# Edge-scoring stage of a graph and expert network: earlier source gathers, and duplicate search and weight sums outside the edge loop

## What is computed

```python
x1 = x[edges[0]]
x2 = x[edges[1]]
e = jnp.concatenate([x1, x2], axis=1) @ Ww + bw
e = e.reshape(-1, H, 2 * HD).transpose(1, 0, 2)
e = jax.nn.leaky_relu(e, 0.01)
w = (e @ Wa + ba)[..., 0]
mat = jnp.full((H, n, n), -jnp.inf, jnp.float32)
mat = mat.at[:, edges[0], edges[1]].set(w)
mat = jax.nn.softmax(mat, axis=-1)
```

## Time and profile before

| | |
|---|---|
| median of 3 runs | 830.37 us (829.98 to 833.03) |
| profiled execution, own time | 826.04 us |
| its span, first to last instruction | 824.3 us |
| PE / DVE / POOL busy | 77% / 62% / 25% of the span |
| granted TensorE clock, mean | 0.864 of full speed |
| DMA moved | 208.07 MB, mean 252 GB/s |

### The profile page before, as it was taken

The page is one execution under the profiler, slowest core; times in us unless marked ns, Lnnn a source line. Parts: engine busy times, 40 slices in busy tenths (PEclk is TensorE's granted clock), DMA queues, the critical chain, the costliest instruction groups (busy, mean ns, idle before and its releaser), DMA issues.

```text
span 824.3 us, 9492 instructions
## 1 busy us (share of the span) xinstructions
PE 637.2 (77%) x2879; PEld 317.8 (39%) x2879; DVE 507.3 (62%) x1437; ACT 252.8 (31%) x1072; POOL 202.8 (25%) x223
## 2 busy tenths in 40 slices
PE   4972345533334938998989999889999999999966
PEld 2431112211113934455455545444444444444422
DVE  3377999889887997547473244774449644443512
ACT  2104776555662332345232010211111111211211
POOL 6047677777772000000000000011101101101100
PEclk9995556755555878999999999999999999999998
DMA  8688878787875709704000002378999999999981
GB/s 330 248 309 319 299 253 261 251 261 261 260 252 195 249 29 410 249 1 154 0 1 1 0 0 77 125 325 357 422 421 421 420 421 423 420 423 421 422 362 42
DMA packets 46645, 208.07 MB, mean 252 GB/s; under 512 B 7969, under 2 KB 12577, under 8 KB 37120
## 3 DMA queue, kind: packets, MB, share of 16 engines
q1 hardware_dynamic: 27296, 145.70, 43.7%
q0 software_dynamic: 19296, 61.75, 22.1%
HBM read 199.67 MB, written 10.31 MB: 255 GB/s over the span
## 4 chain that ended last, share of the span: by engine, by line
PE 60%; DMA 14%; DVE 13%; POOL 5%; issue 5%; ACT 2%; SPq 0%; POOLq 0%; DVEq 0%
PE bank L853 14%; PE bank L543 8%; PE bank L873 6%; PE bank L891 5%; DMA score<-late,e_i 4%; PE bank L741 4%; PE bank L756 4%; DVE R L1324 3%; PE bank L657 3%; POOL R L454 2%; PE bank L650 2%; DMA R<-L_w 2%; DMA R<-tok_tab,slot_tok 2%; DMA R<-tab_src,e_i 2%; POOL R L447 2%
## 5 line engine op out<-in xcount | busy, mean ns | idle before, releaser
L992 ACT ACTIVATE R<-R 128x128 f32<-128x128 f32 x384 | 113.0, 295 | 98.7 <-DVE R L1328 98.7
L591 PE MATMUL bank<-R 128*128 128x384 bf16 x144 | 50.5, 486 | 117.3 <-DVE R L1287 117.3
L853 PE MATMUL bank<-R 128*64 128x512 f32 (+1 forms) x432 | 107.2, 611 | 9.5 <-DMA R<-L_w 8.4
L496 POOL DMA_INDIRECT R<-tok_tab,slot_tok x33 | 33.0, 1000 | 248.7 <-DVE slot_f L1711 203.2
L1723 DVE TENSOR_TENSOR R<-R,bank 128x256 f32<-128x256 f32 x34 | 14.3, 421 | 109.0 <-ACT R L1105 109.0
L543 PE MATMUL bank<-R,late 128*128 128x512 f32 x168 | 77.4, 620 | 2.2 <-DMA R<-L_Ww 2.2
L992 ACT ACTIVATION_READ_ACCUMULATOR R<-R 128x1 f32 x384 | 71.6, 186 | 0.0
L591 PEld LDWEIGHTS bank<-R 128*128 128x128 bf16 x144 | 13.3, 119 | 149.9 <-DVE R L1287 140.9
L1324 DVE TENSOR_TENSOR R<-R 128x1032 f32<-128x1032 f32 x48 | 59.1, 1232 | 17.2 <-DMA R<-tab_src,e_i 10.5
L485 POOL MEMSET R<- 128x512 f32 x3 | 1.6, 525 | 242.4 <-DVEq L1642 242.3
L1328 DVE SCALAR_TENSOR_TENSOR R<-R,sm 128x1024 f32<-128x1024 f32 x48 | 59.1, 1231 | 1.7
(11 more groups left out here) (374 smaller groups left out, 1093.4 us busy)
## 6 DMA issues: line engine op xcount, KB each, us to landing
R<-L_w SPq DMA_DIRECT2D x54, 1536.0 KB, 15.1
late<-L_w SPq DMA_DIRECT2D x18, 1536.0 KB, 15.3
R<-L_w SPq DMA_DIRECT2D x2, 3072.0 KB, 15.4
score<-R POOLq DMA_DIRECT2D x9, 512.0 KB, 12.3
R<-L_Ww SPq DMA_DIRECT2D x2, 2048.0 KB, 13.9
R<-L_W SPq DMA_DIRECT2D x4, 1024.0 KB, 9.2
R<-score SPq DMA_DIRECT2D x2, 1536.0 KB, 10.9
tab_src<-R SPq DMA_DIRECT2D x3, 516.0 KB, 3.8
```

Source lines behind the costliest of these rows:

```text
L496: pool.indirect_dma_start(out=xg[j], out_offset=None, in_=tok_tab[:, :], in_offset=bass.IndirectOffsetOnAxis(ap=slot_tok[:, i:i + 1], axis=0),
L591: last = pe.matmul(pb[s][:, 0:N], oh[:, e % 2, 0, P * s:P * s + P], oh[:, e % 2, 1, :], start=(e == 0), stop=(e == ET - 1))
L853: last = pe.matmul(pb[4 + i % 2][part, :], xeT[i % 2][:, k, part], w13[e % NWB][:, k, :], start=(k == 0), stop=(k == KD - 1), tile_positio ...
L992: act_.activation(own, own, ACT.Copy, accum_out=w_e3[:, t, h:h + 1]).then_inc(S("heads_summed"), 1)
```

## The change

Five more source buffers come out of the `late` tiles (`NGF` = 18), and 16 source gathers (`NEARLY`) are issued ahead of the wait for the destination table. The key products and the duplicate search become functions, `keys(g)` and `seek_duplicates(g)`. Groups 0 and 1 are done within the source table's first tile, groups 2 to 4 between the destination table and the loop, groups 5 to 11 in the loop as before. The two weight sums stand after the counts. The buffer that serves as source for filling the score matrix is now the eighteenth.

```diff
--- before.py
+++ after.py
@@ -32,8 +32,9 @@
 ROUND = 1.5 * 2.0 ** 23
 SLOPE = 0.01
 ROW = 2 * D + H
-NGF = 13
-NEARLY = 9
+NGF = 18
+NEARLY = 16
+DUP_TABLE, DUP_EARLY = 2, 5
 NGD = 6
 V_FROM = 4
 NWB = 11
@@ -149,6 +150,7 @@
         lsc = prod[0]
         ab = [R2[:, 2560 + ROW * j:2560 + ROW * j + ROW] for j in range(NT)]
         ga = [r1(10240 + ROW * j, ROW) for j in range(7)] + [R2[:, 12288 + ROW * j:12288 + ROW * j + ROW] for j in range(6)]
+        ga += [late[0][:, ROW * j:ROW * j + ROW] for j in range(3)] + [late[1][:, ROW * j:ROW * j + ROW] for j in range(2)]
         gd = [r1(ROW * j, ROW) for j in range(NGD)]
         mt = [r1(3072 * j, 3072).rearrange("p (n h) -> p n h", h=H) for j in range(NT)]
 
@@ -550,6 +552,15 @@
 
             pe.wait_ge(S("consts_ready"), 1)
 
+            def keys(g):
+                if g >= 2:
+                    pe.wait_ge(S("dup_used"), g)
+                for j in range(4):
+                    e, o = 4 * g + j, pb[6 + g % 2][:, P * j:P * j + P]
+                    pe.matmul(o, src_h[:, e:e + 1].to_broadcast([P, P]), ident16[:, 0:P], start=True, stop=False)
+                    last = pe.matmul(o, dst_h[:, e:e + 1].to_broadcast([P, P]), ident16[:, P:2 * P], start=False, stop=True)
+                last.then_inc(S("key_psum"), 1)
+
             for t in range(NT):
                 transposes("1", t).then_inc(S("xT_psum"), 1)
             for t in range(NT):
@@ -560,26 +571,23 @@
                     if t:
                         pe.wait_ge(S("src_half_ready"), 2 * (t - 1) + half + 1)
                     project(t, 3 + half, xT, Ww[:, 0:4, D * half:D * half + D]).then_inc(S("src_rows_psum"), 1)
+                    if t == 0:
+                        if half == 0:
+                            pe.wait_ge(S("edge_idx_ready"), 1)
+                        keys(half)
             pe.wait_ge(S("Ww_loaded_dst"), 32)
             for t in range(NT):
                 for half in range(2):
                     if t:
                         pe.wait_ge(S("dst_half_ready"), 2 * (t - 1) + half + 1)
                     project(t, (5, 0)[half], xT, Ww[:, 4:8, D * half:D * half + D]).then_inc(S("dst_rows_psum"), 1)
-            pe.wait_ge(S("edge_idx_ready"), 1)
+            for g in range(DUP_TABLE, DUP_EARLY):
+                keys(g)
             pe.wait_ge(S("src_half_ready"), 2 * NT)
             pe.wait_ge(S("dst_half_ready"), 2 * NT)
             for e in range(ET):
-                if e % 4 == 0:
-
-                    g = e // 4
-                    if g >= 2:
-                        pe.wait_ge(S("dup_used"), g)
-                    for j in range(4):
-                        o = pb[6 + g % 2][:, P * j:P * j + P]
-                        pe.matmul(o, src_h[:, e + j:e + j + 1].to_broadcast([P, P]), ident16[:, 0:P], start=True, stop=False)
-                        last = pe.matmul(o, dst_h[:, e + j:e + j + 1].to_broadcast([P, P]), ident16[:, P:2 * P], start=False, stop=True)
-                    last.then_inc(S("key_psum"), 1)
+                if e % 4 == 0 and e // 4 >= DUP_EARLY:
+                    keys(e // 4)
                 if e % 4 == 2 and V_FROM <= e // 4 < V_FROM + NT:
                     v = e // 4 - V_FROM
                     if v == 0:
@@ -1261,10 +1269,32 @@
                     ins = ts(share, share, bias, None, ALU.add)
                 ins.then_inc(ready, 1)
 
+            dup_scr, dup0_f = dup_s, V_("dup0_f", ET // 4)
+
+            def seek_duplicates(g):
+                t = 4 * g
+                dve.wait_ge(S("key_psum"), g + 1)
+                keys = pb[6 + g % 2]
+                for j in range(4):
+                    e = t + j
+                    lo = P * (j - 1) if j else 0
+                    go(stt(dup_scr[:, 256 * j:256 * j + P * (j + 1) - lo], keys[:, lo:P * (j + 1)], key_f[:, e:e + 1],
+                           before_s[:, 0:2 * P] if j else tri, ALU.is_equal, ALU.mult, accum_out=dup_f[:, e:e + 1]))
+                if g:
+                    go(stt(dup_scr[:, P:2 * P], pb[7 - g % 2][:, 3 * P:4 * P], key_f[:, t:t + 1], ones,
+                           ALU.is_equal, ALU.mult, accum_out=dup0_f[:, g:g + 1]))
+                    settle()
+                    go(tt(dup_f[:, t:t + 1], dup_f[:, t:t + 1], dup0_f[:, g:g + 1], ALU.add))
+                settle()
+                stt(row_i[:, t:t + 4], dup_f[:, t:t + 4], 262144.0, key_f[:, t:t + 4], ALU.mult, ALU.add).then_inc(S("dup_used"), 1)
+                dve.wait_ge(S("dup_used"), g + 1)
+
             for t in range(NT):
                 for half in range(2):
                     dve.wait_ge(S("src_half_ready"), 2 * t + half + 1)
                     linear_part(ab[t], half, S("src_rows_ready"))
+                    if t == 0:
+                        seek_duplicates(half)
             for t in range(NT):
                 dve.wait_ge(S("src_rows_stored"), 16 * NT)
                 dve.wait_ge(S("Ww_loaded_dst"), 32)
@@ -1273,8 +1303,9 @@
                     tt(ab[t][:, D * half:D * half + D], pb[(5, 0)[half]][:, :], bwr[:, D * half:D * half + D], ALU.add).then_inc(S("dst_half_ready"), 1)
                     dve.wait_ge(S("dst_half_ready"), 2 * t + half + 1)
                     linear_part(ab[t], half, S("dst_rows_ready"), bar)
-            dup_scr = dup_s
-            wabs, dup0_f = V_("wabs", 2), V_("dup0_f", ET // 4)
+            wabs = V_("wabs", 2)
+            for g in range(DUP_TABLE, DUP_EARLY):
+                seek_duplicates(g)
 
             def add_linear(t):
                 dve.wait_ge(S("heads_summed"), H * (t + 1))
@@ -1286,35 +1317,14 @@
                 go(ts(oh[:, t % 2, 0, :], iota_h[:, :], src_f[:, t:t + 1], None, ALU.is_equal))
                 ts(oh[:, t % 2, 1, :], iota_h[:, :], dst_f[:, t:t + 1], None, ALU.is_equal).then_inc(S("onehot_ready"), 1)
                 settle()
-                if t % 4 == 0:
-
-                    g = t // 4
-                    dve.wait_ge(S("key_psum"), g + 1)
-                    keys = pb[6 + g % 2]
-                    for j in range(4):
-                        e = t + j
-                        lo = P * (j - 1) if j else 0
-                        go(stt(dup_scr[:, 256 * j:256 * j + P * (j + 1) - lo], keys[:, lo:P * (j + 1)], key_f[:, e:e + 1],
-                               before_s[:, 0:2 * P] if j else tri, ALU.is_equal, ALU.mult, accum_out=dup_f[:, e:e + 1]))
-                    if g:
-                        go(stt(dup_scr[:, P:2 * P], pb[7 - g % 2][:, 3 * P:4 * P], key_f[:, t:t + 1], ones,
-                               ALU.is_equal, ALU.mult, accum_out=dup0_f[:, g:g + 1]))
-                        settle()
-                        go(tt(dup_f[:, t:t + 1], dup_f[:, t:t + 1], dup0_f[:, g:g + 1], ALU.add))
-                    settle()
-                    stt(row_i[:, t:t + 4], dup_f[:, t:t + 4], 262144.0, key_f[:, t:t + 4], ALU.mult, ALU.add).then_inc(S("dup_used"), 1)
-                    dve.wait_ge(S("dup_used"), g + 1)
+                if t % 4 == 0 and t // 4 >= DUP_EARLY:
+                    seek_duplicates(t // 4)
                 if t % 4 == 3 and V_FROM <= t // 4 < V_FROM + NT:
                     v = t // 4 - V_FROM
                     dve.wait_ge(S("Wv_loaded"), 64)
                     dve.wait_ge(S("V_psum"), v + 1)
                     go(dve.tensor_copy(V[v][:, :, HD], ones[:, 0:H]))
                     tt(V[v][:, :, 0:HD], pb[3 + v][:, :].rearrange(heads, h=H), bvr.rearrange(heads, h=H), ALU.add).then_inc(S("V_ready"), 1)
-                if t == 32:
-
-                    dve.wait_ge(S("bit_w_loaded"), 32)
-                    dve.tensor_reduce(wabs[:, 0:1], wu, AX, ALU.add, apply_absolute_value=True).then_inc(S("bit_abs_ready"), 1)
-                    dve.tensor_reduce(wabs[:, 1:2], wd, AX, ALU.add, apply_absolute_value=True).then_inc(S("bit_abs_ready"), 1)
                 j = t % NGF
                 if t == 0:
                     dve.wait_ge(S("first_src_rows"), 16 * NEARLY)
@@ -1347,6 +1357,10 @@
             for t in range(NT):
                 go(ts(xn3[:, t, :], xn3[:, t, :], 1.0, None, ALU.subtract))
                 go(tt(x3[:, t, :], x3[:, t, :], b0r, ALU.add))
+
+            dve.wait_ge(S("bit_w_loaded"), 32)
+            dve.tensor_reduce(wabs[:, 0:1], wu, AX, ALU.add, apply_absolute_value=True).then_inc(S("bit_abs_ready"), 1)
+            dve.tensor_reduce(wabs[:, 1:2], wd, AX, ALU.add, apply_absolute_value=True).then_inc(S("bit_abs_ready"), 1)
 
             nmax = V_("nmax", 24)
             dis, dinv, wsc, half_sc = V_("dis", 3), V_("dinv", 3), V_("wsc", 2), V_("half_sc", 4)
```

## The result

The changed kernel takes 824.29 us (median of 4 runs, 822.98 to 825.67) against 830.65 us of the kernel before (829.98 to 833.03): ratio 0.9907, 95% interval 0.9878 to 0.9937. The forecast was 822.9 us, in 817.5 to 829.5.

What follows compares the result with a forecast made beforehand. POOL's indirect-DMA issues were taken to bound the edge loop, with its start on the destination table and its stalls. Later restart +4.4, seven fewer issues -9.9, fewer stalls -2.0: -7.5 us, 830.37 to 822.9 us, range 817.5 to 829.5.

Steps and rivals of the forecast that it cites:

- The slip of the table phase: Key products of groups 0 and 1 delay PE's path to both tables by 0.9 us.
- The restart: POOL goes on after the third destination store at 66.55 us against 62.13: +4.4 us, bounds +1.1 and +4.8.
- DVE's searches hide: Between the tables and the loop, three searches and the one-hots end at 69.0 us, under the first add's wait.
- The first add: DVE's first edge-loop add, needing 16 source gathers and destination gather 0: 70.9 us by latency, 73.8 at most by traffic.
- Seven issues at 1.42 us, and half of the stalls gone: After the destination table, POOL's seven fewer issues give -9.9 us and fewer stalls -2.0 us; iteration 14 at 114.0 us.
- The searches as cover: Searches left in the first 14 iterations would put DVE at 116.6 us, so moving them is worth 2.6 us.
- Nothing changes from iteration 14 on: In the rest of the edge loop both kernels issue the same three per tile, so no gain or loss.
- The sums behind the loop cost nothing: Two weight sums after the loop end before the read-back's second half lands at 263.38 us: cost 0.
- The sum: Whole kernel: 4.4 - 9.9 - 2.0 = -7.5 us, median from 830.37 to 822.9 us.
- Rival 1: DVE sets the pace until iteration 14, with an early store and no stalls: gain 11.7 us, 818.7 us; chance 0.13.
- Rival 2: Gain mostly given back to DMA: store takes 7.3 us, stalls stay or grow: -3.5 us, 826.9 us; chance 0.24.
- Rival 3: Gathers starve the destination stores, POOL goes on at 74.7 us: +2.6 us, 833.0 us; chance 0.08.

Runs made afterwards that it cites:

- the halves: Early gathers alone (kernel before plus this): 830.33 us, ratio 0.9998; searches and sums alone (changed kernel with 9 early gathers): 828.53 us, ratio 0.9974.

## Why the prediction was right, and where its steps were not

**The slip of the table phase**, +0.9 us: the last table row ends at 58.68 + 0.23 where it ended at 58.23 + 0.23, 0.45 us. One such pair proves little, since the start of the gathers scatters by several microseconds. Better: the first and the third source store are 13.7 to 13.8 us apart in the three traces of the table above with all searches in the loop, and 14.1 to 14.2 us in the three others, so at least 0.4 us are real. What slips ahead of the first store is not shown.

**The restart**, 66.55 us: it came at 65.97. The store took 6.8 us where I had taken 6.9 from the earlier trace rows, and not 3.38 from the third store alone. Counted from the first source gather the loss is 3.1 us on average; the forecast's 4.4, less the slip, is 3.5.

**DVE's searches hide**: the one-hots behind them ended at 68.5 us (69.0 worked out), 4.2 us before the first add.

**The first add**, 70.9 us by latency, 73.8 by traffic at most: 72.72. The gather queued behind those ahead of it. I had the bound, but used the latency.

**Seven issues at 1.42 us, and half of the stalls gone**, iteration 14 at 114.0: it came at 116.85. Here is the step that failed: "POOL by itself gets there" after 32 issues at a fixed 1.42 us, and POOL is "the later one". The 32 issues took 1.49 us each with their gaps, 2.2 us more. The stalls were 3.3 us for 2.0: the 2.2 us for scatters are what was forecast, and 1.05 us for DVE's first scores were not. POOL and DVE are not two chains of which the later counts. DVE makes the adds of tiles 0 to 14 without a pause, from 72.72 to 114.43 us, and from iteration 9 on each scatter ends at a fixed distance behind one of them, so a pair of issues takes 3.00 us, DVE's own pitch of 2.94 and 0.06 us. The forecast's test of whether DVE can follow was the right question, but its answer treated an issue as a fixed cost. Two of its own signs of being wrong came: an issue time over 1.45 us and a wait of POOL for DVE.

**The searches as cover**, worth 2.6 us: the gathers alone reach iteration 14 3.5 us later, counted from the restart. Right, somewhat more. By the medians searches and sums together are worth more still, 5.8 us beside the early gathers (830.33 against 824.52).

**Nothing changes from iteration 14 on**: wrong by 2.6 us. The same 87 issues take 1.39 us with their gap in both traces of the changed kernel, 1.39 and 1.40 in those of the halves, and 1.36 and 1.35 before. In the first trace of before 27 issues start during an add and take 1.25 us, in the changed one 29 take 1.29. That shows where the time sits; why the rhythm falls less well on the adds is open.

**The sums behind the loop cost nothing**: L1374 still ends its wait with the read-back. Right.

**The sum**, -7.5 us: the medians show -6.4 and -6.3. But from the first source gather to the last scatter the forecast amounts to -8.4 us (-7.5 without the slip of 0.9 ahead of that gather), and the traces show -4.0. So the loop's gain was taken at twice its size, through the two steps above: 2.8 us up to iteration 14 and 2.6 after it, less 1.0 that the restart and the tail gave back. That the number on record was near the medians is in part luck. It needs some 2 us of gain that the traces can't place; the two profiled executions of each kernel average 828.2 and 823.7 us, 4.5 us apart, while the two of the kernel before alone differ by 4.4 us.

**The rivals.** Rival 1 was right that DVE sets the pace up to iteration 14, but not in how: it let POOL wait for DVE's scores, which from the measured first add would have given iteration 14 at 111.7 us (its 109.9 and 1.8 more). The scores were ready by then; the held-up issues were not in it. Its early store and missing stalls didn't come either. Rival 2 had the store at 7.3 us (6.8 and 6.95 came), but the stalls did not grow over those of before. Rival 3's store, starved until 74.7 us, didn't come.

## What to carry to other kernels

An indirect DMA issued by GpSimd is not a fixed cost where VectorE works beside it: look at whether issues end at a common distance behind VectorE's instructions with two SBUF operands before multiplying a mean by a count. And a wait that the profile puts down to a score is a wait for it only if the score came after the engine had gone idle: of three such waits in the changed kernel two were none. Work taken from one of two engines locked like that was worth little alone, in either direction: the two halves gave 0.0% and 0.3% (within noise), together 0.8 to 0.9%. And the landing time of a store is that of its new company: three stores with gathers in flight took 6.7 to 7.5 us, where the third had taken 3.4 with the gathers drained.

## What was not expected of the hardware

A GpSimd DMA issue that starts during a VectorE add of two SBUF operands ends 0.81 to 0.93 us after the add, up to 2.08 us in all against 0.94 to 1.04 us beside neither long operation; with one operand in PSUM it takes 0.94 to 1.03 us beside the add. VectorE itself loses only 0.06 us, in the operation that starts with the issue (L1312, 0.22 in place of 0.16 us). A copy with one SBUF operand seems to do the same. The last scatter of the changed kernel starts within L1348 and ends 0.86 us after it; it takes 1.22 us where the last scatter of before, started 0.08 us behind the end of the same copy, took 0.98:

```profile
251.35 0.76 DVE L1348 COPY late<-late 128x1152 f32<-128x1152 f32 x1
...
251.75 1.22 POOL L463 DMA_INDIRECT score<-late,e_i  x1 [0.67 <-issue]
```

And on two of three chips ScalarE paused up to 3.1 us at a time between instructions of the same loop. The kernel before takes some 845 us on those two and 831 on the other; how much of that the pauses make is not shown.
